# Gathering rows of x·W1 in place of rows of x in the first edge stage of a two-layer graph network

## What is computed

```python
def _mlp(h, W, b, gamma, beta):
    h = h @ W + b
    mu, var = jnp.mean(h, axis=0), jnp.var(h, axis=0)
    h = (h - mu) * jax.lax.rsqrt(var + EPS) * gamma + beta
    return h * jax.nn.sigmoid(h)
msg  = _mlp(concatenate([x[src], edge_attr], axis=1), W1, b1, g1, be1)   # 400,000 x 128 @ 128 x 64
agg  = segment_sum(msg, dst) / max(count(dst), 1)
x1   = layernorm(x + _mlp(concatenate([x, agg], axis=1), W2, b2, g2, be2))
msg  = relu(x1[src] + edge_attr)                                          # second layer
x2   = layernorm(x1 + relu((x1 + segment_sum(msg, dst)) @ W.T + b))
```

## Time and profile before

| | us |
|---|---|
| median of three runs | 10092.78 (10090.55 to 10096.55) |
| the profiled execution | 10097.42 |
| its span, first to last instruction | 10095.6 |

### The profile page before, as it was taken

How to read it: one execution, slowest core, us unless ns; L and a number is a source line. 1 busy time by engine, 2 the same in 40 slices (tenths; PEclk the granted TensorE clock), 3 DMA queues, 4 the chain that set the end, 5 groups by cost and what they waited for, 6 DMA issues and landing times. The chain is left out here.

```text
span 10095.6 us, 84004 instructions
## 1 busy us (share of the span) xinstructions
PE 4342.8 (43%) x22658; PEld 2749.4 (27%) x22658; DVE 1862.2 (18%) x4868; ACT 1238.3 (12%) x2056; POOL 5961.9 (59%) x6272
## 2 busy tenths in 40 slices
PE   3434343433434344347974333333433433333335
PEld 1222222222222222226872222222222222222222
DVE  2111111111111111116763000000000000000002
ACT  0000000000000000004663000000000000000001
POOL 6666666666666666661003666666666666666662
PEclk7666666666666666668986666666666666666666
DMA  3222222222222222224551121211211211111111
GB/s 80 68 66 69 67 67 66 69 67 66 69 65 69 66 69 67 66 69 131 170 150 49 45 45 45 45 45 45 46 45 45 46 45 46 45 45 45 45 45 33
DMA packets 800215, 638.45 MB, mean 63 GB/s; under 512 B 532451, under 2 KB 618703, under 8 KB 799368
## 3 DMA queue, kind: packets, MB, share of 16 engines
q1 hardware_dynamic: 553308, 326.50, 12.0%
q0 software_dynamic: 200416, 208.55, 10.8%
q10 hardware_dynamic: 46400, 102.52, 3.1%
HBM read 528.15 MB, written 108.90 MB: 63 GB/s over the span
## 5 line engine op out<-in xcount | busy, mean ns | idle before, releaser
L1196 POOL DMA_INDIRECT X<-x_scratch,src_idx x3125 | 2968.6, 950 | 1632.2 <-issue 884.4
L371 POOL DMA_INDIRECT Z<-in_x_dram,src_idx x3125 | 2963.0, 948 | 1619.5 <-issue 899.1
L416 PE MATMUL PS<-ZT,W_sb 128*64 128x320 f32 x2500 | 1196.7, 620 | 2717.0 <-ACT ZT L456 2386.8
L1218 PE MATMUL PS<-hot_c,msg_c 128*64 128x48 f32 x6250 | 661.3, 271 | 2768.0 <-issue 1637.2
L1218 PEld LDWEIGHTS PS<-hot_c,msg_c 128*64 128x64 f32 x6250 | 577.0, 184 | 3166.3 <-issue 2044.2
L416 PEld LDWEIGHTS PS<-ZT,W_sb 128*64 128x64 f32 x2500 | 396.5, 185 | 3156.8 <-issue 2371.1
L522 DVE BATCH_NORM_STATS2 stats<-PS 128x320 f32 (+1 forms) x624 | 279.4, 490 | 3673.6 <-remote 3416.8
L456 ACT ACTIVATE ZT<-PS 128x640 f32<-128x640 f32 x625 | 423.0, 702 | 4155.5 <-remote 3280.1
L1254 DVE TENSOR_TENSOR table<-table,PS 64x48 f32 x625 | 130.2, 208 | 4043.4 <-DMA shares_scratch<-counts 3418.0
L1237 ACT ACTIVATE msg_c<-PS 128x320 f32<-128x320 f32 x625 | 261.4, 436 | 4298.0 <-DMA counts_scratch<-table 3058.7
L1207 PE MATMUL PS<-E,ident 128*128 128x320 f32 x1250 | 688.8, 643 | 11.9 <-DMA E<-in_edge_attr_dram 11.9
(11 more groups left out here) (135 smaller groups left out, 2517.7 us busy)
## 6 DMA issues: line engine op xcount, KB each, us to landing
Z<-in_edge_attr_dram SPq DMA_DIRECT2D x625, 160.0 KB
E<-in_edge_attr_dram SPq DMA_DIRECT2D x625, 160.0 KB
h_scratch<-h_ring ACTq DMA_DIRECT2D x312, 320.0 KB
hT<-h_scratch SPq DMA_DIRECT2D x312, 320.0 KB
Z<-in_x_dram,src_idx POOLq DMA_INDIRECT x3125
X<-x_scratch,src_idx POOLq DMA_INDIRECT x3125
x_nodes<-in_x_dram SPq DMA_DIRECT2D x1, 3125.0 KB
x_ring<-in_x_dram SPq DMA_DIRECT2D x25, 125.0 KB
```

The costliest lines, as they stand in the source:

```text
L371: nc.gpsimd.indirect_dma_start(out=Z[:, r, j, 0:D], out_offset=None, in_=x, in_offset=bass.IndirectOffsetOnAxis(ap=src_idx[:, n:n + 1], ax ...
L416: nc.tensor.matmul(PS[ab * D:(ab + 1) * D, bank + c, 0:HC], W1_sb[:, :], ZT[:, s % 2, c * HC:(c + 1) * HC], start=True, stop=True)
L1196: nc.gpsimd.indirect_dma_start(out=X[:, r, j, :], out_offset=None, in_=x1_dram, in_offset=bass.IndirectOffsetOnAxis(ap=src_idx[:, n:n + 1] ...
L1218: last = nc.tensor.matmul(PS[D:P, 2 + s % S, 0:WIN], msg[:, s % S, j, :], hot[:, s % S, j, :], start=(j == 0), stop=(j == TG - 1))
```

## The change

The preparation makes `y = x @ W1[0:64]` for all nodes and stores it; the first stage gathers rows of y. For that x is loaded in five pieces, ahead of the target indices; PE turns two 125 x 128 pieces at a time, ACT copies them to `xT`, PE multiplies them with `Wx` (W1's upper half twice on the diagonal), DVE copies the result to `y_nodes` (25 rounds), and SP stores it in five DMAs. POOL's first gather waits for all five stores.

In the stage the edge features of two groups (a pair) lie side by side in `E` (5 pairs) and are turned and copied to `ET` two pairs ahead of the product; the product of the pair with `We` (W1's lower half twice on the diagonal) opens a sum in PSUM, and the gathered rows `Y` (5 pairs) are added to it by products with slices of the identity. PE counts once for a turned pair (`e_turned`) and once for a finished pair (`dense_done`). POOL waits for every second group only, and for a finished pair.

```diff
 # preparation
                         sp.dma_start(src_rows[:, :], src_v).then_inc(s_src, 16)
+                        for n in range(XLOADS):                     # XLOADS = 5
+                            sp.dma_start(x_nodes[:, n * XC:(n + 1) * XC],
+                                         x_v.rearrange("p t c -> p (t c)")[:, n * XC:(n + 1) * XC]).then_inc(s_x[n], 16)
                         sp.dma_start(dst_rows[:, :], dst_v).then_inc(s_dst, 16)
                         sp.dma_start(base_in[:, :], first_v, allow_slow_non_contiguous=True).then_inc(s_first, 16)
-                        sp.dma_start(x_nodes[:, :], x_v.rearrange("p t c -> p (t c)")).then_inc(s_x, 16)
+                        for n in range(XLOADS):
+                            sp.wait_ge(y_taken, QUADS // XLOADS * (n + 1))   # QUADS = 25
+                            sp.dma_start(y_v[:, n * XC:(n + 1) * XC], y_nodes[:, n * XC:(n + 1) * XC]).then_inc(y_stored, 16)
...
+                        turn_x(0)                                   # PE
+                        for c in range(QUADS):
+                            if c + 1 < QUADS:
+                                turn_x(c + 1)
+                            pe.wait_ge(xT_taken, c + 1)
+                            if c >= 2:
+                                pe.wait_ge(y_taken, c - 1)
+                            for a in range(2):
+                                last = nc.tensor.matmul(PS[0:NP, 6 + c % 2, a * P:(a + 1) * P], xT[:, c % 2, a, :],
+                                                        Wx[:, :], start=True, stop=True)
+                            last.then_inc(y_put, 1)
 # first gather stage: SP
-                        for s in range(slots):
-                            wait_at(sp, rows_done, k, BODY, s + 1 - RING)
-                            sp.dma_start(Z[:, s % RING, :, D:2 * D], edge_v[at(k, BODY, s)]).then_inc(e_loaded[s % RING], 16)
+                        for q in range(-(-slots // 2)):
+                            wait_at(sp, e_turned, k, 10, q + 1 - S)         # S = 5
+                            for s in range(2 * q, min(2 * q + 2, slots)):
+                                sp.dma_start(E[:, q % S, :, s % 2, :],
+                                             edge_v[at(k, BODY, s)]).then_inc(e_loaded[q % S], 16)
 # POOL
+                    pool.wait_ge(y_stored, 16 * XLOADS)
+                    carry_wait(pool)
                     for g in range(G):
                         r = g % RING
-                        if g >= RING:
-                            pool.wait_ge(rows_done, g + 1 - RING)
+                        if g >= RING and g % 2 == 0:
+                            pool.wait_ge(dense_done, g // 2 + 1 - S)
                             carry_wait(pool)
                         for j in range(TG):
                             nc.gpsimd.indirect_dma_start(
-                                out=Z[:, r, j, 0:D], out_offset=None, in_=x,
+                                out=Y[:, r // 2, j, r % 2, :], out_offset=None, in_=y_dram,
 # PE
+                    def turn_edges(k, q, alone):
+                        parts = D if alone else P
+                        wait_at(pe, et_taken, k, 10, q - 1)
+                        pe.wait_ge(e_loaded[q % S], at(k, 64, 32 * (q // S) + (16 if alone else 32)))
                         for j in range(TG):
+                            last = nc.tensor.transpose(banks(2 * (q % 2), 2, parts, EG)[:, j * P:(j + 1) * P],
+                                                       E[:, q % S, j, :, :].rearrange("p a c -> p (a c)")[:, 0:parts],
+                                                       ident[:, :])
+                        last.then_inc(e_turned, 1)
+
+                    def dense(k, q, alone):
+                        pe.wait_ge(et_taken, at(k, 10, q + 1))
+                        wait_at(pe, h_ready, k, 10, q - 1)
                         for c in range(2):
+                            nc.tensor.matmul(PS[0:parts, bank + c, 0:HC], We[0:parts, 0:parts],
+                                             ET[0:parts, q % S, c * HC:(c + 1) * HC], start=True, stop=False)
+                        for s in range(2 * q, 2 * q + (1 if alone else 2)):
+                            pe.wait_ge(gathered[s % RING], at(k, 32 * TG, 16 * TG * (s // RING) + 16 * TG))
+                        for j, c, first, cols in ((0, 0, 0, P), (1, 0, P, P), (2, 0, 2 * P, D),
+                                                  (2, 1, 0, D), (3, 1, D, P), (4, 1, D + P, P)):
+                            at_col = c * HC + first - j * P
+                            nc.tensor.matmul(PS[0:parts, bank + c, first:first + cols],
+                                             Y[:, q % S, j, :, :].rearrange("p a c -> p (a c)")[:, 0:parts],
+                                             ident[:, at_col:at_col + cols], start=False, stop=first + cols == HC)
+                        ... (the one-hot counts of both groups)
+                        last.then_inc(dense_done, 1)
+
+                    turn_edges(0, 0, False); turn_edges(0, 1, False)
+                    # for each pair q: turn_edges(q + 2), dense(q)
 # ACT
+                    def take(k, q, parts):
+                        act.wait_ge(e_turned, at(k, 10, q + 1))
+                        wait_at(act, dense_done, k, 10, q + 1 - S)
+                        act.activation(ET[0:parts, q % S, :], banks(2 * (q % 2), 2, parts, EG),
+                                       ACT.Copy).then_inc(et_taken, 1)
+                    # for each pair q: take(q + 2), store(q - 1)
 # DVE: one-hots are made two pairs ahead, pair(q) waits for dense_done q + 1
```

More of the change, by code:

```diff
@@ L148, in gnn_kernel @@
         flag = sb(ctx, "flag", [1, 1], int32)
-        W1_sb = sb(ctx, "W1_sb", [2 * D, D])
+        Wx = sb(ctx, "Wx", [P, P])
+        We = sb(ctx, "We", [P, P])
         W2_sb = sb(ctx, "W2_sb", [2 * D, D])
@@ L217, in take_indices @@
                                          put[:, :, 0:SB])
-        s_x = sem("s_x")
+        XLOADS = 5
+        XC = NT // XLOADS * D
+        s_x = [sem(f"s_x{n}") for n in range(XLOADS)]
+        y_stored = sem("y_stored_x")
         s_w = sem("s_w")
@@ L334, in gnn_kernel @@
             count_added = sem("count_added")
-            e_loaded = [sem(f"e_loaded{r}") for r in range(RING)]
+            e_loaded = [sem(f"e_loaded{q}") for q in range(S)]
             gathered = gathered_x
-            rows_done = sem("rows_done")
-            zt_taken = sem("zt_taken")
+            e_turned = sem("e_turned")
+            et_taken = sem("et_taken")
             dense_done = sem("dense_done")
@@ L418, in dense @@
-                        if alone:
-                            nc.tensor.matmul(PS[D:P, bank, 0:HC], W1_sb[:, :], ZT[:, s % 2, HC:2 * HC],
-                                             start=True, stop=True)
-                        pe.wait_ge(hot_ready, at(k, BODY, s + 1))
-                        for j in range(TG):
-                            last = nc.tensor.matmul(PS[0:D, bank + ab, HC:HC + WIN], ones_bf[:, :],
-                                                    hot[:, q % 5, ab, j, :], start=(j == 0), stop=(j == TG - 1))
+                            nc.tensor.matmul(PS[0:parts, bank + c, 0:HC], We[0:parts, 0:parts],
+                                             ET[0:parts, q % S, c * HC:(c + 1) * HC], start=True, stop=False)
@@ L425, in dense @@
+                        pe.wait_ge(hot_ready, at(k, BODY, 2 * q + (1 if alone else 2)))
+                        for ab in range(1 if alone else 2):
+                            for j in range(TG):
+                                last = nc.tensor.matmul(PS[0:D, bank + ab, HC:HC + WIN], ones_bf[:, :],
+                                                        hot[:, q % 5, ab, j, :], start=(j == 0), stop=(j == TG - 1))
                         last.then_inc(dense_done, 1)
                     def body(k, slots):
-                        for s in range(slots):
-                            if not (slots < BODY and s == slots - 1):
-                                turn_rows(k, s + 1)
-                            dense(k, s, slots < BODY and s == slots - 1)
@@ L433, in _ @@
-                    turn_rows(0, 0)
+                        for q in range(-(-slots // 2)):
+                            if slots == BODY or q + 2 <= slots // 2:
+                                turn_edges(k, q + 2, slots < BODY and q + 2 == slots // 2)
+                            dense(k, q, slots < BODY and q == slots // 2)
+                    turn_edges(0, 0, False)
+                    turn_edges(0, 1, False)
                     all_bodies(pe, body)
@@ L450, in store @@
                                       h_ring[:, q % 5, :]).then_inc(h_stored[q % 5], 16)
-                    def body(k, slots):
-                        for s in range(slots):
-                            act.wait_ge(rows_done, at(k, BODY, s + 1))
-                            wait_at(act, dense_done, k, BODY, s - 1)
```

(17 more changed lines are left out.)

78 lines of the change are left out of this document (52 added, 26 removed).

## The result

The changed kernel takes 10115.88 us (median of 11 runs, 10111.82 to 10125.27), the kernel before in 11 runs beside it 10094.19: a ratio of 1.0024, 95% interval 1.0016 to 1.0032. It is slower by 22 us, where 10045 was predicted. The profiled execution of after took 10125.27, 9.4 above its median; its span is 27.8 longer than before's.

What follows compares the result with a forecast made beforehand. The prediction took POOL's gather queue, with 648 us of stops, to bound the first gather stage. Start +53, POOL's wait -101 and the rest 0 gave -48 from 10092.8, so 10045 us, range 9820 to 10150.

Steps and rivals of the forecast that it cites:

- The start: Preparation: POOL's first gather waits for the stores of y and moves by +53 us, bounds +25 and +60.
- The length of the runs: First gather stage: POOL issues 40 gathers between stops in place of 20, as four increments still get through per restart.
- the 0 that the prediction put on TensorE inside the stage: First gather stage: TensorE's changed work costs 0, within 4 us either way, being hidden behind POOL.
- 31 in place of 28 x 2: First gather stage: TensorE's matmuls per pair were given as 31 after the change and 28 x 2 before.
- The size of the term: POOL's wait in the first gather stage: stops fall from 655 to 554 us, -101, bounds 0 and -648.
- the prediction's own line: POOL's stops: one after n gathers lasts 1.29 + 0.145 n us; the stage loses 3125 x (0.145 + 1.29 / n).
- The law of the stops: First gather stage: stops grow with the run before them, 648 us in all, on top of 1.25 us per gather.
- the rival that they don't: First gather stage: any stop costs 4.19 us, so 78 cost 327; -321 + 53 gives 9825 us; chance 0.13.
- nearly no change: First gather stage: runs of 25 to 34 gathers win 40 to 83 us against +53; 10063 to 10106; chance 0.17.
- Runs don't get longer: First gather stage: increments pass only just after a restart, runs stay at 20, 0 won, +53; 10146 us; chance 0.20.
- Tail 0: After the last gather: five pairs take about as long as ten groups did, about 20 us, so 0.
- I take nothing: Start of the first stage: preparing target indices after the barrier costs 0, beside the first ten groups' gathers (62.5 us).

Runs made afterwards that it cites:

- e3: The changed kernel with two more TensorE increments per pair, on a semaphore nobody waits for, and no instruction more; 10116.7 us, kernel before beside it 10091.8.
- e2: The changed kernel with four of five count columns left out, 23 matmuls per pair in place of 31, same increments; 10073.9 us, kernel before beside it 10091.8.
- e8: The changed kernel with both groups' counts made in one matmul of 96 columns, 26 matmuls per pair in place of 31; 10039.9 us, kernel before 10043.4.
- f3: The changed kernel with ten more one-column matmuls per pair, 41 in place of 31, no increment more; 10172.6 us, kernel before beside it 10103.6.
- h1: The changed kernel with a pair's edge half turned and copied just ahead of its own product; 10106.3 us, the changed kernel as its reference 10060.9.
- e5: The changed kernel with POOL setting 900 unread elements and waiting for them after each pair's ten gathers; 10058.3 us, kernel before beside it 10043.4.
- e6: The changed kernel with POOL setting 100 unread elements per partition ahead of every gather; 10074.0 us, kernel before beside it 10043.4.
- f4: The changed kernel with first-stage gathers of 64 rows in place of 128, same number of gathers; 10128.4 us, kernel before beside it 10103.6.
- g2: The changed kernel with split preparation transfers, merged counts, and in the second stage VectorE adding the rows and one-hots four groups ahead; ratio 0.9947 to before.
- e1: The changed kernel without making or storing y, the first stage gathering rows of x; 10081.1 us, kernel before beside it 10091.8.

## Why the prediction was wrong, step by step

- **The start: right.** +53 was predicted, 54.8 measured; the stores of y ran at 128 GB/s (predicted about 120) up to the first gather at 84.26 (82.4). The reason given holds too: the rounds on the engines were done at 46, and the stores behind the loads on SP's queue came last.
- **The length of the runs: wrong, and this is the step that failed.** "I take 40 because it only carries over the count of increments": 24.2 was measured. The count of increments does nothing (e3). What is charged in this stage is TensorE's small matmuls by their number (e2, e8, f3), and the number of matmuls went up from 28 to 31 per pair. With it falls the 0 that the prediction put on TensorE inside the stage, "hidden behind POOL". The prediction's "31 in place of 28 x 2" is a plain error of count: 10 turns, 8 passes and 10 counts are 28 for the pair, and x8668 in the earlier trace rows says so. It reads as if TensorE's matmuls were nearly halved when their number grew.
- **The size of the term.** Predicted -101, measured -25.2. By the prediction's own line 24.2 gathers a run are worth -35 and not -101. The stops did fall by 34 (648 to 614), and some 8 us went back into the gathers themselves, whose busy time alone rose from 2963.0 to 2969.7. As to the cause: three matmuls more are +14; against it stand the 37 to 40 by which before lies above the line, which the work ahead of the product would explain (h1, without it, gives 35 back). -38 + 14 = -24, by an estimate; that the 38 are due to that distance alone is not shown.
- **The law of the stops: right as a reading, wrong as a cause.** It gives 5.64 for 30 gathers and 9.99 for 60; measured about 5.7 and 10.1. So stops do grow with the run, against the rival that they don't. But it made POOL's 1.25 per gather the floor and the stops the loss. e5, e6 and f4 show stops and POOL's own time exchanged for each other; the floor of 3906 was not one. And it is not one of the gathers alone: in before's second stage, where the prediction reads n = 26 off the line, POOL stopped once in 22.3 gathers, for which the line gives 634 and not the 602 read; and g2 has runs of 38.6 there without the gain.
- **The rivals.** The nearest is "nearly no change", runs of 25 to 34 and 10063 to 10106; the 24.2 and 10115.88 lie just outside it. "Runs don't get longer" named the right place, work that gets through only behind a restart, but put it on the increments.
- **Tail 0: right.** From the last gather to the aggregate 20.7 (4621.20 to 4641.89).
- "I take nothing" for the target indices is right for this kernel; e1 shows some 15 us as soon as y doesn't cover them.

Sum on the profiles: +54.8 - 25.2 - 1.8 = +27.8; on the medians +21.7.

## What to carry to other kernels

Where an idle engine is read as waiting, look at its own pace first: one matmul in 1 to 2 us with "issue" ahead of it is an engine held up, and what paid in the first stage here was to cut the number of its matmuls, not their columns or its increments (in the second stage eight fewer per pair brought nothing). Count instructions per unit before and after from the trace's own counts. And before a busy queue is taken as the bound, make it a little slower and a little faster: if the stage takes the same, the bound is elsewhere.

## What was not expected of the hardware

While POOL issued indirect gathers without a pause TensorE fell, some 10 us after a restart, from 5.5 matmuls per us to 0.7, with its increments 15 us late; it came free when POOL stopped. The stage took 1.45 us per gather whether POOL needed 1.205, 1.25 or 1.31 for one, and 13 to 17 ns more for each small matmul, of 1, 48 or 96 columns. What the shared path is stays open. It is not the fetching of instructions: the queue that the profile calls "instruction" moved nothing between 2040 and 2067, and in the whole run no more than this (packets, MB, share of 16 engines' time):

```profile
q14 instruction: 73, 0.60, 0.0%
```

The Trainium skill, "NOTIFIC — the notification-queue block", section "Overflow: three behaviours, one of which stalls the engine", says that the block that carries the records of instructions holds its sources back rather than lose a record. A price per matmul that hardly depends on its width would fit that; no run here can show it, since each was recorded.
